# Order of masks, of a Silu slot and of the end of a lone cross attention in a fused decoder kernel

## The reference

```python
x = x + _L0_attn_ref(_layernorm(x), ...)   # 4 layers: causal linear attention (16 heads), layernorm, GELU network, layernorm
x = x + _L0_xattn_ref(_layernorm(x), ctx)  # cosine similarity with a context
x = x + _L0_ffn_ref(_layernorm(x), ...)    # top 2 of 8 gates, two Silu experts counted
x = x + _L1_attn_ref(_layernorm(x), ...)   # state space block: conv, 512 x 16 states scanned over time, quantised decay
x = x + _L1_xattn_ref(_layernorm(x), ctx)  # cross attention, 8 heads of 64
x = x + _L1_ffn_ref(_layernorm(x), ...)    # 8 experts, top 2, capacity 512 slots each, GELU
```

## Time and profile before

| what | value |
|---|---|
| runs of before | 2347.54 us, 2353.7 us, 2344.39 us; median 2347.54 |
| the profiled execution, its own time | 2350.0 us |
| its span | 2348.2 us |
| busy share of the span | PE 87%, PEld 53%, DVE 74%, ACT 42%, POOL 13% |
| mean granted TensorE clock | 0.935 of full speed |

### The profile page before, as it was taken

How to read it: one execution, slowest core, us unless ns; L and a number is a source line. 1 busy time by engine, 2 the same in 40 slices (tenths; PEclk the granted TensorE clock), 3 DMA queues, 4 the chain that set the end, 5 groups by cost and what they waited for, 6 DMA issues and landing times.

```text
span 2348.2 us, 29854 instructions
## 1 busy us (share of the span) xinstructions
PE 2035.5 (87%) x10638; PEld 1242.1 (53%) x10638; DVE 1731.6 (74%) x2590; ACT 989.5 (42%) x1531; POOL 306.1 (13%) x338
## 2 busy tenths in 40 slices
PE   6999989998999999885668887988788889859998
PEld 4666656665666666552323343534354445646665
DVE  7777767777777778869999899989898997331111
ACT  1222222222222222237665876577667883312221
POOL 1111111111111111110000000000000000231222
PEclk9999999999999999998779988988889999869999
DMA  9000000000000100002110111011101113012442
GB/s 246 1 0 19 28 26 1 18 28 26 1 14 14 50 1 1 1 9 67 61 59 21 36 43 60 4 36 60 36 18 37 61 54 113 33 49 65 124 123 53
DMA packets 64498, 99.66 MB, mean 42 GB/s; under 512 B 12036, under 2 KB 47391, under 8 KB 64368
## 3 DMA queue, kind: packets, MB, share of 16 engines
q1 hardware_dynamic: 58416, 90.14, 12.1%
q0 software_dynamic: 5952, 7.86, 1.7%
HBM read 83.57 MB, written 15.60 MB: 42 GB/s over the span
## 4 chain that ended last, share of the span: by engine, by line
PE 54%; DVE 30%; issue 10%; ACT 4%; POOL 1%; DMA 0%; DVEq 0%; ACTq 0%; POOLq 0%
PE po L1861 9%; PE pa L1851 9%; DVE arena L1592 8%; PE pa L2444 5%; PE po L2455 4%; DVE arena L1582 4%; PE pa L2133 3%; PE pa L1788 2%; DVE arena L1159 2%; PE pa L1900 2%; PE pa L1841 2%; DVE arena L1600 2%; DVE arena L1161 2%; PE pt L1826 1%; PE pt L1834 1%
## 5 line engine op out<-in xcount | busy, mean ns | idle before, releaser
L2133 PE MATMUL pa<-arena 128*128 128x512 f32 x512 | 301.4, 718 | 81.4 <-DVE arena L1600 81.0
L1592 DVE TENSOR_TENSOR_SCAN arena<-arena 128x1024 f32<-128x1024 f32 x128 | 292.4, 2284 | 19.5 <-ACT arena L929 19.3
L581 POOL TENSOR_SCALAR arena<-arena 128x2 f32<-128x2 f32 (+2 forms) x93 | 27.7, 298 | 1534.0 <-DVE arena L1440 823.9
L1861 PE MATMUL po<-arena 128*128 128x256 f32 x960 | 221.1, 382 | 0.0
L1851 PE MATMUL pa<-arena 128*128 128x512 f32 x480 | 212.3, 594 | 3.7 <-ACT arena L751 3.4
L2133 PEld LDWEIGHTS pa<-arena 128*128 128x128 f32 x512 | 101.5, 217 | 212.4 <-DVE arena L1600 108.0
L1233 DVE TENSOR_TENSOR arena<-pa,arena 128x512 f32<-128x512 f32 x256 | 158.7, 682 | 64.5 <-PE pa L1788 64.4
L913 ACT ACTIVATE arena<-arena 128x510 f32<-128x510 f32 x256 | 170.4, 716 | 53.6 <-DVE arena L1592 49.8
L1861 PEld LDWEIGHTS po<-arena 128*128 128x128 f32 x960 | 176.9, 189 | 28.1 <-issue 3.0
L736 ACT COPY arena<-po 128x512 f32<-128x512 f32 x32 | 18.7, 586 | 361.6 <-PE po L1773 361.6
L1582 DVE TENSOR_TENSOR arena<-arena 128x1024 f32<-128x1024 f32 x128 | 154.7, 1208 | 7.5 <-PE pa L2133 4.5
(11 more groups left out here) (284 smaller groups left out, 3715.8 us busy)
## 6 DMA issues: line engine op xcount, KB each, us to landing
arena<-bc_rows SPq DMA_DIRECT2D x64, 512.0 KB, 4.2
arena<-in_L_ffn_W SPq DMA_DIRECT2D x16, 1024.0 KB, 7.8
arena<-in_L_attn_W SPq DMA_DIRECT2D x8, 1024.0 KB, 5.2
arena<-rows_to_experts SPq DMA_DIRECT2D x8, 520.0 KB, 9.4
rows_to_experts<-arena SPq DMA_DIRECT2D x4, 1024.0 KB, 13.7
out<-arena SPq DMA_DIRECT2D x5, 512.0 KB
arena<-in_x SPq DMA_DIRECT2D x4, 512.0 KB, 6.9
arena<-in_rows SPq DMA_DIRECT2D x8, 256.0 KB, 3.2
```

The source lines that it names most:

```text
L1592: v.tensor_tensor_scan(h.rearrange(flat), decay.rearrange(flat), h.rearrange(flat), 0.0, ALU.mult, ALU.add).then_inc(scan_done, 1)
L1861: last = mm(po[s][:, ts(i, D)], gT[:, c, ts(tile, P)], w2[:, c, :], start=c == 0, stop=c == FM - 1)
L2133: last = mm(pa[c][:, :], ident, uh[i % len(uh)][:, n, :], start=g == 0 and n == 0, stop=g == NS // NG - 1 and n == NG - 1)
```

## The change

It reorders instructions; none is added, and three filler matmuls of `kept_busy` go. In four parts:

- In the 15 bodies with both halves, `mask_scores(3)` moves ahead of `ffn_normalised(0)` on VectorE.
- In the mixer the Silu moves from slot 19 to 20, and all that follows in the head by one or two slots: additions to 21 and 22, statistics 23, scaling 24, transposes 25 and 26, copies 27 and 28, `in_half(0)` 28. For the head that stands alone only the numbers change.
- In the lone cross attention the addition of tile 2 moves behind the minimum of unit 15 (slot 30), its statistics behind that; `last_scaled` of the three tiles moves behind the division of tile 3. TensorE finishes tile 3 up to its output projection first and only then turns the three tiles for the router; `ranks` of the three tiles goes behind the router of the last; the copies and scalings on ACT and DVE follow that order.
- The paced sends of GpSimd wait for one weighing less each (12 where it was 13 at the most).

```diff
@@ -663,7 +663,7 @@
                 if places == 1:
-                    pool.wait_ge(av2_done, 16 * (PAIRS - 1) + min(i + 5, 13))
+                    pool.wait_ge(av2_done, 16 * (PAIRS - 1) + min(i + 4, 12))
                 for k in range(2):
@@ -803,7 +803,7 @@
                 gelu(i)
-            for i in (12, 13, 15, 19, 25, 26):
+            for i in (12, 13, 15, 20, 27, 28):
                 head(i)
@@ -867,10 +867,10 @@
                     gate_exp()
-                if i == 19:
+                if i == 20:
                     experts_silu()
-                if i in (25, 26):
-                    rows_out(i - 10, i - 25)
+                if i in (27, 28):
+                    rows_out(i - 12, i - 27)
@@ -991,11 +991,10 @@
                         top_gates(0, LAST_THREE, 1)
-                    if i == 35:
-                        last_rows_out(1, po[1][:, :], 0, 2)
-                        last_rows_out(2, pt[1][:, 0:S], 2, 1)
+                last_rows_out(1, po[1][:, :], 0, 2)
+                last_rows_out(2, pt[1][:, 0:S], 2, 1)
+                last_rows_out(3, po[1][:, 0:S], 3, 1)
                 top_gates(LAST_THREE, LAST_TILE, 2)
-                last_rows_out(3, po[1][:, 0:S], 3, 1)
                 top_gates(LAST_TILE, NT, 3)
@@ -1263,11 +1262,11 @@
                 ffn_residual(0)
-                for i in (16, 17, 19, 20):
+                for i in (16, 17, 21, 22):
                     head(i)
                 ffn_normalised(0)
-                head(21)
-                head(22)
+                head(23)
+                head(24)
                 ffn_residual(1)
@@ -1304,10 +1303,10 @@
                 divide(0)
+                mask_scores(3)
             if ffn:
...
             if attn:
-                mask_scores(3)
                 divide(1)
@@ -1521,15 +1520,15 @@
                     pair_biased(i - 14)
-                if i == 19:
+                if i == 21:
                     pair_added(0)
                     pair_added(1)
-                if i == 20:
+                if i == 22:
                     pair_added(2)
                     pair_added(3)
-                if i == 21:
+                if i == 23:
                     statistics(rows_of(n))
-                if i == 22:
+                if i == 24:
                     scaled(head_groups[2], rows_of(n), xnt).then_inc(xn_ready, 1)
@@ -1547,7 +1546,7 @@
                                     sm[:, tile, :].unsqueeze(2).broadcast_to([P, QH, QD]), ALU.mult).then_inc(at2_ready, 1)
-                if i % 8 == 3 + drain and i >= 11 + drain:
+                if i == 30 if at.lone and 28 < i < 32 else i % 8 == 3 + drain and i >= 11 + drain:
                     tile = (i - 11 - drain) // 8
@@ -1640,10 +1639,8 @@
                     early_routing(i - 1)
-                    if i == 30:
+                    if i == 31:
                         last_statistics(0, TT - 1)
-                    if i == 31:
-                        last_scaled(1, 0, TT - 1)
             if q is not None:
@@ -1671,17 +1668,18 @@
             if at.lone:
+                last_scaled(1, 0, TT - 1)
+                cross(UNITS + 3 + drain)
+                last_statistics(TT - 1, TT)
                 last_logits(q + 1, pt[1], LAST_THREE, LAST_TILE)
...
                 compared(LAST_THREE, LAST_TILE)
+                last_scaled(2, TT - 1, TT)
                 counted(LAST_THREE, LAST_TILE)
                 chosen(LAST_THREE, LAST_TILE)
-                cross(UNITS + 3 + drain)
-                last_statistics(TT - 1, TT)
                 weighed(LAST_THREE, LAST_TILE, 2)
...
                 placed(LAST_THREE, LAST_TILE)
-                last_scaled(2, TT - 1, TT)
                 last_logits(q + 2, pt[0], LAST_TILE, NT)
@@ -2006,8 +2004,8 @@
             down(3)
-            head(23)
-            head(24)
+            head(25)
+            head(26)
@@ -2116,9 +2114,9 @@
                     expert_pair(i - 13)
-                if i in (23, 24):
-                    rows_transposed(i - 8, i - 23, 3)
-                if i == 26:
+                if i in (25, 26):
+                    rows_transposed(i - 10, i - 25, 3)
+                if i == 28:
                     pe.wait_ge(head_a, HEAD_A * n + HEAD_A)
@@ -2285,7 +2283,7 @@
                     cross(i)
-                if n is not None and (p is not None or i == UNITS - 6):
+                if n is not None and (p is not None or i == UNITS - 4):
                     head(i)
@@ -2307,25 +2305,24 @@
             if at.lone:
+                cross(UNITS + 1)
+                cross(UNITS + 2)
+                kept_busy(po[0], 1)
+                for i in range(UNITS + 3, UNITS + 4 + 2 * ahead):
+                    cross(i)
                 pe.wait_ge(at2_ready, 4 * q + TT - 1)
...
                 last_rows(pt[1], 2, 1)
-                cross(UNITS + 1)
                 kept_busy(po[0], 1)
-                cross(UNITS + 2)
                 last_router(2, pt[1], 0, TT - 1)
-                for i in range(UNITS + 3, UNITS + 4 + 2 * ahead):
-                    cross(i)
-                kept_busy(po[0], 1)
-                ranks(LAST_THREE, LAST_TILE, 2)
-                kept_busy(po[0], 3)
                 pe.wait_ge(xr_ready, q + 2)
...
                 last_router(3, pt[0], TT - 1, TT)
+                ranks(LAST_THREE, LAST_TILE, 2)
                 ranks(LAST_TILE, NT, 3)
...
             if q is not None:

```

## The result

The change makes the kernel faster: 2314.3 us is the median of its four runs (2313.4 to 2324.1), against 2346.3 us for the four of before on the same chip. The ratio is 0.9859, with a 95% interval from 0.9834 to 0.9883: 33.1 us less, give or take 5.7. Two more measurements of the same kernel on other chips gave 0.9870 (0.9846 to 0.9893) and 0.9837 (0.9814 to 0.9861), so 30.6 and 38.3 us less. I had forecast 27.0 less, 2320.5, with a range from 2314 to 2334: the direction and the three mechanisms hold, and the sum came out 6 us too small.

The account below looks back on a forecast made before the run. No single engine sets the time (TensorE 54% of the chain, VectorE 30%), so each stage was priced separately: 17.5 + 2.8 + 6.7 = 27.0 us off 2350.0 gives 2323.0, or 2320.5 against the median; range 2314 to 2334.

Parts of the forecast that it names:

- the three mechanisms: Masks ahead of the normalisation -17.5 us, Silu at slot 20 -2.8, reordered end of the lone cross attention -6.7.
- the projection behind the transposes of slot 19: Mixer bodies with cross attention: TensorE's projection there taken at 3.32 us as in slot 11, not 1.90.
- Masks: 15 attention bodies: project(0) no longer waits 1.21 us for the mask of tile 3; -17.5 us in all.
- `state_weighed(1)` ends at 426.38: Attention body shown: project(0) starts at 426.38 instead of 427.59, at that record's end.
- The bound of -20.3: Attention bodies: most the moved mask could win, from VectorE's idle 1.35 us in 15 bodies.
- Silu: Two mixer bodies with cross attention: exponentials ahead of the Silu win 2.1 us each, less 0.7 at slot 27; -2.8.
- The price at slot 27: Mixer: with in_half(0) moved to slot 28, slot 27's projection could take 1.42 us longer; half, 0.7 a body, was taken.
- Rival 1: Mixer: the Silu's gain goes back at slots 20 and 27; part two 0, total 2323.3 us; chance 0.17.
- End: Lone cross attention: first send 4.85 us earlier, no gap before the last sends 1.85 more; -6.7 us.
- the gap ahead of the last sends: Lone end: GpSimd's 2.15 us wait for the last places after six sends goes, worth 1.85 us.
- Rival 2: Lone cross attention: the end wins little, TensorE slow through it; -2.2 us, total 2325.0; chance 0.12.
- Rivals 3 and 4: Attention bodies: next body takes 1.21 us back, 2338.0, chance 0.08; GpSimd stretches VectorE's normalisation, 2351.5, chance 0.03 within, 0.02 beyond.

Follow-up runs that it names:

- e1: Only the attention bodies' mask_scores(3) moved ahead of the normalisation, against the kernel before; ratio 0.9902 (0.9875 to 0.9929), 23.0 us less.
- e11: The change as it is, measured a third time, against the kernel before; ratio 0.9837 (0.9814 to 0.9861).
- e3: Only the reordered end of the lone cross attention with its paced sends, against the kernel before; ratio 0.9983 (0.9967 to 0.9999), 4.0 us less.
- e4: The whole change again, on the same chip as its three parts, against the kernel before; ratio 0.9870 (0.9846 to 0.9893), 30.6 us less.
- e12: The change with the attention bodies' second division also ahead of the normalisation; against the kernel before, ratio 0.9982 (0.9968 to 0.9997), 4.2 us less.
- e7: The change with the three tiles' rows and router ahead of tile 3's projection again; against the kernel before, ratio 0.9830 (0.9809 to 0.9851), 40.0 us less.
- e9: The change plus one filler matmul ahead of the scores of unit 1 of the lone cross attention; against the kernel before, ratio 0.9824 (0.9801 to 0.9847).

## Why the prediction fell short

The mechanisms held and terms were mis-sized. The step that failed most is the clock of TensorE in the mixer: the prediction took the projection behind the transposes of slot 19 as slow in every body and put the part at 2.8 us, and it put the lone cross attention ahead of tile 2's projection at nothing, without a reason. The traces show 4.6 us at the moved steps and 2.9 us in that later stretch.

**Masks: the mechanism right, the term mis-sized, 17.5 against 18.9** (the mean first scan of the ten traces with the mask moved and the normalisation ahead of the division, 1074.8, against 1093.7 in the three without). The step is "`state_weighed(1)` ends at 426.38", taken as when `project(0)` can start. In the trace of after, `project(0)` starts at 420.10, 0.44 us behind the start of `state_weighed(1)` and 0.17 ahead of the end of its record. And matmuls that don't start behind a wait are quicker: 1.90 and not 2.00 for `project(0)`, and `weigh(3)` starts 1.83 behind it and not 1.94. 1.21 + 0.17 + 0.11 is 1.49; the body gained 1.45 up to `project(1)`. That body is near the upper end: 18.9 over fifteen is 1.26 each, and the ordinary ones gained 1.15 to 1.50 in e1. The Trainium skill (Perfetto Trace Analysis, Summary: the profiler window per engine type) says that a matmul's reported end is an estimate; the rows of this case agree, with 0.17 us of overlap. Over the thirteen bodies between GpSimd's copies the change saves 17.3 us in e11. The bound of -20.3 from VectorE's idle 1.35 was too tight by the same rows, if barely: VectorE's two divisions are 5.21 us apart now and were 6.64.

**Silu: the mechanism right, the term mis-sized, 2.8 forecast, 4.6 at the moved steps.** The two bodies whole differ by 5.8 (485.4 against 491.2 us) and the stretch behind them by 2.9 (102.9 against 105.9 to tile 2's projection), as means over traces. The other 1.2 of the 5.8 lie in units where nothing was edited and where either order scatters by 5 us, so they can't be laid to the change. I had set the projection behind the transposes of slot 19 as slow in every body, as slot 11 has it; ten of 22 have it so (2.82 to 3.24 us) and gain 2.0 to 3.0, and twelve have it at full clock (1.90) and gain 3.75. The price at slot 27 was put at 0.7 a body and is 0.92, but by another row than I named: the projection of slot 27 never slows down (1.90 in all 22), it starts late, because the clock fell in slots 25 to 27. The rule of the Trainium skill (TensorE: Matmul & The Clock Gate, HAM oscillation), that gaps between bursts bring the throttle back, is borne out in kind, in seven of 22 bodies that have `in_half(0)` later and in none of six that have it in slot 26. Six are few: with a share of 7 in 22 none of six would be slow in one case of ten, so that the later `in_half(0)` is the cause is likely but not shown. That a fixed place would be slow was my reading of the page and is wrong. The 2.9 us behind the bodies were in no term. Rival 1, that the Silu's gain goes back, is right for 0.92 of 3.23.

**End: 6.7 forecast, 7.3 without the stall, 1.2 to 2.4 with it.** Step by step against e11, in us counted from the start of tile 2's projection: division done at 6.2 forecast and 5.9 measured, logits 13.3 and 12.3, first send 22.1 and 21.4, and the gap ahead of the last sends worth 1.85 forecast and 10.93 - 9.11 = 1.82 measured. With the stall the division is done at 9.1 to 11.0 and the logits at 17.7 to 18.9: 2.7 us of standing, then weighings and projection mostly near half clock (1.97, and 2.2 to 3.1 for the projection). The stall is in four of the ten traces that have the new end (the first, e3, e4, e12). It is always at this place, and the addition then starts 3.8 to 4.0 us behind the projection's start. In the six others and in the four traces with the old end it starts 1.94 behind it.

**The sum** from means over the traces is 18.9 + 5.8 + 2.9 + 7.3, or 1.5 with the stall for the last, so 35 or 29 us. Three chips measured 33.1, 30.6 and 38.3, each give or take over 5; the last is above the sum and within its interval of it. That the total came within 6 us of the forecast is in part luck: the prediction knew neither of the stall, which takes 5 to 6 us, nor of the 2.9. Rival 2, "the end wins little", is what four of ten traces show, at its price of 2.2, but the reason I gave came second: the stall opens the idle time in which the clock falls. Rivals 3 and 4 have nothing for them. No body took the gain back, and the moved scalings take 0.73, so GpSimd does not stretch them.

**Why the first profile was slow** follows from the same table: 2322.3 against e11's 2312.7 is 7.8 us in the two bodies and 6.0 at the end, less 3.0 in the first stage and 1.4 in the rest. All of the first two is clock and stall in identical code. So one profile of this kernel can't price a part to better than about 8 us in all, and its parts must be read by what the rows say, not by the span.

**What stays open.** What ACT and VectorE wait for in the stall. Both wait for TensorE alone, whose rows are done, and they go on within 0.1 us of each other. Of instruction fetches, the DMA view has one packet near this place in each of the ten traces with the new end: 7.8 to 9.2 us behind the projection's start in the four with the stall, 8.7 in e7, 3.3 to 5.1 in the other five. In the four it comes after the stall is over, so it isn't that. Nor is it the paced sends alone, which run beside that place in the traces without it too. Whether the old end is free of it is not shown either: at four in ten, none in four traces comes about in one case of eight by luck. Also open is why the clock comes back earlier in the lone cross attention when the slots are new. Neither was tried further. No version beats the change by a margin that was measured: e9, whose one filler does nothing known, has 0.9824 against 0.9837 beside it, with intervals of 0.0023 either way.

## What to carry to other kernels

When a wait is taken away, price it from start to start, not from the end of the record ahead of it: `project(0)` starts 0.17 us before that end, and over fifteen bodies the whole miss was 1.4 us. A step moved ahead of a wait must leave enough behind it to fill the wait, as the normalisation does for the masks (59.3 us a body) and does not once the division is ahead of it (61.6). Where an engine's clock falls and comes back, read the same place in several bodies and several traces, and put a price with its share of cases on it, since one body is a sample of one.

## What the hardware did that was not expected

- The same instructions behind the same idle time of 1.85 us ran at full clock in one body and near half in the next (1.99 and 3.78 us for four matmuls, granted clock 1.00 and 0.53). Behind 2.95 us of idle time the clock was back after 6.6 us in one kernel and not yet after 9.9 in another.
- Six fillers in slots 22 to 24, 2 us of dense matmuls per slot, did not keep the clock from falling in slots 25 to 27 (12.73 us from scan 27 to 29 in one of two bodies).
- A stall that makes VectorE 1.9 to 2.1 us and ACT 3.4 to 3.6 us late, always at one place, in some executions of a kernel and not in others (four of ten traces with the new end), which the profile lays at "remote" in a program of one core.
